# Group 2's second-layer routing and the shared units behind the block loop, and the first page pair's results

## What is computed

```
x = x + attention(ctx, layernorm(x), mask)            # 8 heads, 77 keys
x = x + experts0(layernorm(x))                        # 8 experts, 2 per token, and a shared one
x = x + depool(layernorm(x), ctx): rmsnorm(...) @ W_in.T + b_in + scanned patches
x = x + experts1(layernorm(x))                        # 32 experts, 6 per token, and a shared one

experts1:  scores = sigmoid(x @ gate.T)
           s = scores + bias; the best 4 of 8 groups of experts; then the best 6 experts
           w = 2.5 * scores[best] / sum(scores[best])
           out = sum_e w_e * relu(x @ up_e.T)**2 @ down_e.T + relu(x @ shared_up.T)**2 @ shared_down.T
```

## Time and profile before

| | |
|---|---|
| median of three runs | 887.16 us |
| profiled execution, its own time | 888.47 us |
| its span, first to last instruction | 886.6 us |
| busy: PE, DVE, ACT, POOL | 722.6, 416.7, 273.0, 308.5 us |
| mean granted TensorE clock | 0.903 |
| scatters on POOL: rows_in 96, rows_out 114 | 93.5 and 112.9 us |

### The profile page before, as it was taken

The page is one execution under the profiler, slowest core; times in us unless marked ns, Lnnn a source line. Parts: engine busy times, 40 slices in busy tenths (PEclk is TensorE's granted clock), DMA queues, the critical chain, the costliest instruction groups (busy, mean ns, idle before and its releaser), DMA issues.

```text
span 886.6 us, 14153 instructions
## 1 busy us (share of the span) xinstructions
PE 722.6 (82%) x4526; PEld 631.4 (71%) x4526; DVE 416.7 (47%) x1615; ACT 273.0 (31%) x620; POOL 308.5 (35%) x322
## 2 busy tenths in 40 slices
PE   3868886389999999999899888866776868787865
PEld 2647776289999999999899877533456757676754
DVE  4998664022333243546644742725104444456563
ACT  2636631022111111222223122321123455445540
POOL 1333307600010111100552354172712656556560
PEclk9898859589999999999999998796978899989998
DMA  8999992231776767755866624242646556587866
GB/s 257 396 296 268 257 252 97 102 125 53 231 231 219 218 221 244 246 169 190 304 218 232 217 89 170 92 166 87 217 154 189 177 158 191 164 288 243 285 215 250
DMA packets 93534, 181.22 MB, mean 204 GB/s; under 512 B 9857, under 2 KB 54998, under 8 KB 93182
## 3 DMA queue, kind: packets, MB, share of 16 engines
q1 hardware_dynamic: 78048, 138.67, 50.9%
q0 software_dynamic: 13344, 38.68, 11.6%
q10 hardware_dynamic: 2046, 2.71, 1.0%
HBM read 134.07 MB, written 65.62 MB: 225 GB/s over the span
## 4 chain that ended last, share of the span: by engine, by line
PE 56%; DVE 16%; issue 10%; another core or an unknown queue 6%; DMA 4%; ACT 3%; POOL 3%; SPq 1%; DVEq 0%; POOLq 0%; ACTq 0%
PE PB L618 16%; PE PB L655 11%; PE PB L632 5%; PE PB L825 4%; PE PB L816 4%; PE PB L763 3%; POOL rows_out L1930 3%; PE PB L777 2%; PE PB L804 2%; DMA X<-in_x 2%; PE PB L684 1%; PE PB L600 1%; DMA MEM<-rows_out 1%; DVE WK L1256 1%
## 5 line engine op out<-in xcount | busy, mean ns | idle before, releaser
L618 PE MATMUL PB<-XT,MEM 128*128 128x128 f32 x1584 | 185.9, 276 | 1.1 <-issue 1.1
L618 PEld LDWEIGHTS PB<-XT,MEM 128*128 128x128 f32 x1584 | 181.7, 193 | 1.5 <-issue 1.3
L1882 POOL DMA_INDIRECT sorted_y<-WK x36 | 34.5, 958 | 279.0 <-DVE WK L1470 279.0
L1891 POOL DMA_INDIRECT rows_in<-MEM x96 | 93.5, 974 | 65.1 <-DVE MEM L1674 36.6
L655 PE MATMUL PB<-MEM,WK 128*128 x432 | 99.7, 380 | 3.3 <-DVE MEM L1646 1.9
L825 PE MATMUL PB<-MEM,WK 128*128 x228 | 67.6, 424 | 32.0 <-DVE WK L1823 26.1
L655 PEld LDWEIGHTS PB<-MEM,WK 128*128 128x128 f32 x432 | 79.3, 190 | 13.2 <-issue 3.9
L1930 POOL DMA_INDIRECT rows_out<-WS,MEM x58 | 56.7, 977 | 64.4 <-ACT WS L1045 49.2
L825 PEld LDWEIGHTS PB<-MEM,WK 128*128 128x128 f32 x228 | 42.2, 207 | 41.2 <-issue 36.9
L1930 POOL DMA_INDIRECT rows_out<-MEM x56 | 56.2, 1003 | 40.5 <-ACT MEM L1045 25.7
L939 ACT ACTIVATE XT<-PB 128x256 f32<-128x256 f32 x52 | 19.8, 381 | 162.2 <-PE PB L600 134.2
(11 more groups left out here) (280 smaller groups left out, 1255.4 us busy)
## 6 DMA issues: line engine op xcount, KB each, us to landing
MEM<-in_w SPq DMA_DIRECT2D x36, 896.0 KB
rows_in<-in_consts SPq DMA_DIRECT2D x32, 600.0 KB, 12.2
MEM<-in_w SPq DMA_DIRECT2D x36, 512.0 KB
MEM<-rows_in SPq DMA_DIRECT2D x58, 300.0 KB
MEM<-rows_out SPq DMA_DIRECT2D x16, 768.0 KB, 7.0
MEM<-in_w SPq DMA_DIRECT2D x32, 256.0 KB, 2.8
MEM<-in_w SPq DMA_DIRECT2D x2, 3072.0 KB, 18.9
sorted_x<-MEM SPq DMA_DIRECT2D x1, 5070.0 KB, 39.7
```

Source lines behind the costliest of these rows:

```text
L618: t = e.matmul(o[:, to:to + P], UPW[m][i % (3 - m)][:, k, c * P:(c + 1) * P], XT[:, n % 2, k, :], start=(k == 0), stop=(k == 1))
L1882: e.indirect_dma_start(out=DY, out_offset=bass.IndirectOffsetOnAxis(ap=DEST[:, i:i + 1], axis=0), in_=YS[:, i % 2, :], in_offset=None).the ...
L1891: e.indirect_dma_start(out=DX1, out_offset=bass.IndirectOffsetOnAxis(ap=SLOT1[:, i, j:j + 1], axis=0), in_=XR[:, i, :], in_offset=None).th ...
```

## The change

Four things are changed.

- Group 2's `t1` and `wi` both stand in item i = 34. `t1` stands inside the first part of up, behind two of its seven columns (`SOON`), `wi` behind the seventh; `t2` moves to item 35. Behind the loop `ro 2` now stands directly behind the last block's down and ahead of the late items, and `rank 2`, then DVE's `shares 2` and `slots 2` as entries of their own, around down late 1 and ahead of `sum a 3`. Rank of group 2 uses banks 4 and 5, no longer 2 and 3, so it doesn't wait for "done0".
- q1 and q2 of group 3 are written in halves: two tiles on ACT, two on DVE ("q1v", "q2v").
- Units 4 and 5 are split: "u" is U alone, "d" is D alone, and DVE's drain of unit 3 is an entry of its own ahead of `left 2` and `t2 3`. The pages stand behind entry 8 instead of 7.
- In the pair loop, down2 of pair 0 comes in step 1 instead of 2, and up2 of pair 0, with its relu and square, is first in step 0, ahead of turn1 of pair 1.

With 36 blocks the list is now: turn late 1, down of the last block, ro 2, up late 0, up late 1, down late 0, rank 2, shares 2, down late 1, slots 2, sum a 3, 0, 1, 2, sum b 3, q1 3, 3, t1 3, wi 3, u 4, q2 3, d 3, drain 3, left 2, t2 3, u 5, ro 3, d 4, 6, rank 3, shares 3, 7, slots 3, left 3, 8, pages 3, 9 to 16.

```diff
+ENDS = {s: s - 2 for s in range(2, NPR + 2)}
+ENDS[1] = ENDS.pop(2)
...
+STEP_AT2 = 0, 1, 1, 2, 3, 4
+SOON = {(SUM_AT[2] + 1, 1)}
 for g_ in range(NR - 1):
-    for k_, at_ in enumerate(STEP_AT):
+    for k_, at_ in enumerate(STEP_AT if g_ < 2 else STEP_AT2):
...
-        ("turn", 1), ("down", -1), ("wi", 2), ("up", 0), ("q2", 2), ("up", 1), ("t2", 2), ("down", 0), ("ro", 2), ("down", 1),
-        ("sum a", 3), 0, ("sum b", 3), ("rank", 2), 1, ("q1", 3), 2, ("t1", 3), ("wi", 3), 3, ("left", 2), ("q2", 3),
-        ("t2", 3), 4, ("ro", 3), 5, ("rank", 3), ("left", 3), 6, 7, ("pages", 3), *range(8, 17))
+        ("turn", 1), ("down", -1), ("t2", 2), ("ro", 2), ("up", 0), ("up", 1), ("down", 0), ("rank", 2), ("shares", 2),
+        ("down", 1), ("slots", 2), ("sum a", 3), 0, 1, 2, ("sum b", 3), ("q1", 3), 3, ("t1", 3), ("wi", 3), ("u", 4), ("q2", 3),
+        ("d", 3), ("drain", 3), ("left", 2), ("t2", 3), ("u", 5), ("ro", 3), ("d", 4), 6, ("rank", 3), ("shares", 3), 7,
+        ("slots", 3), ("left", 3), 8, ("pages", 3), *range(9, 17))
...
 def banks_of(g, name):
-    return (4, 5) if g == 2 and name != "rank" else (2, 3)
+    return (4, 5) if g == 2 else (2, 3)
...
                         for c in range(7 - 3 * m):
+                            if m == 0 and c == 2:
+                                between(n, nb, True)
...
             def step(s, n_pairs):
-                if 0 <= s - 2 < n_pairs:
-                    down2(s - 2)
+                if ENDS.get(s, n_pairs) < n_pairs:
+                    down2(ENDS[s])
+                if s == 0:
+                    up2(s)
                 if s + 1 < n_pairs:
                     turn1(s + 1)
                 if 0 <= s < n_pairs:
-                    up2(s)
+                    if s > 0:
+                        up2(s)
...
-                    for i in range(4):
+                    for i in range(4 if g < 3 else 2):
                         t = e.activation(to[:, i, :], X[:, a + i, :], ACT.Identity, bias=R2[:, a + i:a + i + 1],
...
+                if name in ("q1", "q2") and g == 3:
+                    to = XQ if name == "q1" else XR[:, a:b, 0:D]
+                    q.wait_ge("off" + name[1], g)
...
+                    for i in (2, 3):
+                        t = e.tensor_scalar(to[:, i, :], X[:, a + i, :], RS[:, a + i:a + i + 1], R2[:, a + i:a + i + 1],
+                                            ALU.mult, ALU.add)
+                    t.then_inc(*q.mark(name + "v"))
```

More of the change, by code:

```diff
@@ L248 @@
 for nb_ in BLOCKS:
-    k_ = 2
+    k_ = 3
     for i_ in range(BLOCKS[0], nb_):
-        if i_ - SUM_AT[2] >= STEP_AT[k_]:
+        if k_ < 6 and i_ - SUM_AT[2] >= STEP_AT2[k_]:
             EXTRA[nb_, i_] = [(2, k_)]
@@ L255, with steps_of, tail @@
     TAIL[nb_] = [what for what in (
-        ("turn", 1), ("down", -1), ("wi", 2), ("up", 0), ("q2", 2), ("up", 1), ("t2", 2), ("down", 0), ("ro", 2), ("down", 1),
-        ("sum a", 3), 0, ("sum b", 3), ("rank", 2), 1, ("q1", 3), 2, ("t1", 3), ("wi", 3), 3, ("left", 2), ("q2", 3),
-        ("t2", 3), 4, ("ro", 3), 5, ("rank", 3), ("left", 3), 6, 7, ("pages", 3), *range(8, 17))
+        ("turn", 1), ("down", -1), ("t2", 2), ("ro", 2), ("up", 0), ("up", 1), ("down", 0), ("rank", 2), ("shares", 2),
+        ("down", 1), ("slots", 2), ("sum a", 3), 0, 1, 2, ("sum b", 3), ("q1", 3), 3, ("t1", 3), ("wi", 3), ("u", 4), ("q2", 3),
+        ("d", 3), ("drain", 3), ("left", 2), ("t2", 3), ("u", 5), ("ro", 3), ("d", 4), 6, ("rank", 3), ("shares", 3), 7,
+        ("slots", 3), ("left", 3), 8, ("pages", 3), *range(9, 17))
         if not isinstance(what, tuple) or what[1] != 2 or what[0] in rest_
-        or {"q2": "wi", "left": "rank"}.get(what[0]) in rest_]
-def steps_of(n, nb):
+        or what[0] in ("shares", "slots", "left") and "rank" in rest_]
+def steps_of(n, nb, soon=False):
     i = n - EARLY
-    return EXTRA.get((nb, i), ()) if i >= BLOCKS[0] else STEPS.get(i, ())
+    if i < BLOCKS[0]:
+        return [s for s in STEPS.get(i, ()) if (s[0] == 2 and (i, s[1]) in SOON) == soon]
+    if soon:
+        return ()
+    return EXTRA.get((nb, i), ())
 def banks_of(g, name):
-    return (4, 5) if g == 2 and name != "rank" else (2, 3)
-def tail(nb, turn, up, down, mid, up1, down1):
+    return (4, 5) if g == 2 else (2, 3)
+def tail(nb, turn, up, down, mid, up1, down1, drain):
     late = EARLY + nb
@@ L282, in tail @@
                 down(late + i)
+            elif name == "u":
+                up1(i)
+            elif name == "d":
+                down1(i)
+            elif name == "drain":
+                drain(i)
             else:
@@ L635, in up, with between @@
                     between(n, nb)
-            def between(n, nb):
-                for g, k in steps_of(n, nb):
+            def between(n, nb, soon=False):
+                for g, k in steps_of(n, nb, soon):
                     if k in (1, 2, 3, 4) and n + 1 < EARLY + nb + LATE:
@@ L994, in block_iteration @@
                             mid(g, name, 6, 7)
+                    for g, k in steps_of(n, nb, True):
+                        mid(g, NAMES[k], 6, 7)
                     gates(n, nb)
@@ L1035, in act_program, with relu @@
             number1 = e.value_load(PAGES, min_val=0, max_val=P)
+            def relu(s):
+                q.wait_ge("bu", s)
+                q.wait_ge("bd", s - 3)
+                e.activation(HT1[:, s % 3, :, :].rearrange("p b c -> p (b c)"), PB[:, 4 + s % 4, 0:256],
+                             ACT.Relu).then_inc(*q.mark("brl", s))
             def step(s, n_pairs):
-                if 0 <= s - 2 < n_pairs:
-                    r = s - 2
+                if s == 0:
+                    relu(s)
+                if ENDS.get(s, n_pairs) < n_pairs:
+                    r = ENDS[s]
                     q.wait_ge("bd", r)
@@ L1052, in step @@
                                  ACT.Copy).then_inc(*q.mark("bxt", s + 1))
-                if 0 <= s < n_pairs:
-                    q.wait_ge("bu", s)
-                    q.wait_ge("bd", s - 3)
-                    e.activation(HT1[:, s % 3, :, :].rearrange("p b c -> p (b c)"), PB[:, 4 + s % 4, 0:256],
-                                 ACT.Relu).then_inc(*q.mark("brl", s))
+                if 0 < s < n_pairs:
+                    relu(s)
             for s in range(-1, COMMON):
@@ L1737, in page_experts, with drain @@
                 e.tensor_copy(PAGES, EV[0:1, 1:2]).then_inc(*q.mark("pgs"))
-            def down1(n):
+            def drain(n):
                 c, g = UNITS[n]
@@ L1755, in end0, with drain_ahead @@
                     left(n, nb)
-                tail(nb, skip, lambda n: hidden(n, nb), lambda n: result(n, nb), behind_blocks, skip, down1)
+                def drain_ahead(n):
+                    if n != 3:
+                        drain(n)
+                tail(nb, skip, lambda n: hidden(n, nb), lambda n: result(n, nb), behind_blocks, skip, drain_ahead, drain)
             started = len(means)
@@ L1807, in dve_program, with products @@
             running = [None]
+            def products(s):
+                ht = HT1[:, s % 3, :, :].rearrange("p b c -> p (b c)")
+                q.wait_ge("brl", s)
+                e.tensor_tensor(ht, ht, PB[:, 4 + s % 4, 0:256], ALU.mult).then_inc(*q.mark("bh", s))
             def step(s, n_pairs):
@@ L1813, in step @@
                         q.wait_ge(f"w1{j}", 8 * j + 7)
+                if s == 0:
+                    products(s)
                 for k in range(0 if s < 0 else s + 3, min(s + 4, n_pairs)):
```

26 lines of the change are left out of this document (16 added, 10 removed).

## The result

The changed kernel takes 896.97 us (median of 20 runs, 889.37 to 901.09) against 887.93 us for the kernel before in the same comparison (20 runs, 878.86 to 898.59): a ratio of 1.0108, 95% interval 1.0084 to 1.0133. It is slower by 1.1%, outside the range of 868 to 891. The profiled run took 896.35 us, span 894.5 us. Group 3's slots pass the point at which rival D was said to decide, and the unit that part 5 was to gain is lost, as D says; more is lost than D had priced.

What follows compares the result with a forecast made beforehand. The pair loop was taken to start when the shared units are through, which runs of scatters delay by slowing PE. Terms -0.4 - 3.45 - 1.0 = -4.85 against the profiled 888.5 gave 883.65, median 882.3, range 868 to 891.

Steps and rivals of the forecast that it cites:

- rival D: Behind the block loop, group 2's run meets units, turn and product together: slots 7 us later, 889 to 893, chance 0.13.
- part 5: Units behind group 3's slots: PE has one unit more behind the run's start, last unit 3.45 us sooner, or 0.
- part 2: Router and slots of group 2, behind the block loop: slots end at 557.5 instead of 571.6, 14 us sooner.
- part 1: Group 2's turn and product in one block-loop item: loop ends 0.6 us later, bounds 0 and 3.5.
- part 4: Group 2's scatters meet group 3's turn and product: group 3's slots end at 616.9, term 0.4 us, bounds -4 and +8.
- part 6: First pair's products earlier in the pair loop: first scatter 7.1 us behind the turn, 1.0 us gained, bounds 0 and 2.2.
- slow stretch: After 9 to 12 us of back-to-back scatters, PE slows to 1.3 to 1.5 us a matmul until past their end.
- Part 3: Group 3 up to its turn: sums, units and q1 together gain nothing, 0 to 1 us.
- C: Scatters don't slow PE: group 3's product at 576, slots at 598.6, no unit waits; 854 to 870, chance 0.07.
- B: The slow stretch catches less of group 3: its slots end 7 to 12 us sooner, 870 to 876, chance 0.15.
- E: The change does nothing, its gain turned into waiting for the third run's slow stretch: 885 to 889, chance 0.15.

Runs made afterwards that it cites:

- e10: Changed kernel with group 1's last nine scatters held back until group 2's slots are known, then 33 in one run: 905.37 us, ratio 1.0074.
- e1: Changed kernel with POOL's last two runs swapped, group 2's 24 scatters behind group 3's: 902.72 us, ratio 1.013.
- e3: Changed kernel with POOL's two runs behind the block loop broken into gated portions of mostly 3 or 4 scatters: 864.5 us, ratio 0.97.
- e7: e3 with the first run of 32 scatters in portions too: 839.84 us, ratio 0.9458.
- e2: Changed kernel with the 32 expert weight loads cut to 16 of 512 columns: 896.12 us, ratio 1.0068.
- e13: e7 with half of part 6 undone, the first pair's second product back in its old place: 840.39 us, ratio 0.9457.
- e15: e7 measured again, with part 6 as changed: 837.14 us, ratio 0.9403.
- e6: Kernel before, without the change's edits, with POOL's two later runs in portions: 872.66 us, ratio 0.9824.
- e9: e7 without part 6: 840.17 us, ratio 0.9356.
- e11: e9 with gates asking for group 1's last nine scatters in threes; they went as three and six: 840.84 us, ratio 0.937.
- e8: Changed kernel with group 2's 24 scatters back to back but held until group 3's product is through on PE: 896.24 us, ratio 1.0082.
- e12: e6 with part 6 added: 876.79 us, ratio 0.9742.
- after: The kernel with the whole change, against the kernel before: 896.97 us, ratio 1.0108.

## Why the prediction was wrong

Five terms failed: part 2's list of what the stretch meets, which left out nine scatters (8.1 us by e10); part 1's 0.6 us for the end of the loop, which was 4.1; part 4's 21.7 us behind group 3's product, which were 23.7; part 5's gain of 3.45 us, of which nothing came; and part 6's 1.0 us, which no run can tell from nothing.

The profiled run was forecast at 883.65 and is 896.35, 12.7 us more. The slots of group 3 give 5.8 of these (622.7 against 616.9), the units behind them 4.1, the way from the last relu to the first turn 0.6 (9.5 us against 8.9), and the pair loop 2.3 (1.3 longer where 1.0 less was forecast), all rounded.

**The bound and the slow stretch** were right in the main. e1, e3 and e7 show that the late completions follow the runs of scatters, e2 that they don't follow the loads. The 9 to 12 us at pace don't hold for the nine: with the one scatter just before them their run starts at 540.8, and matmuls recorded by 547.1, 6 us into it, are late by 5 us and more (ACT's copy at 552.2 waits 8.3 us). The rule of the Trainium skill ("SBUF — State Buffer", "Who interferes with whom") that TensorE's ports are shared with nobody and a DMA never contends with a compute engine does not account for these traces: scatters alone, spaced out, gave PE 145 matmuls for 104. The runs don't show which resource is shared, so they don't say that the rule on ports is false.

**Part 1** failed in "one wait grows and one goes". The wait for the turn did come, 3.63 us, at the same distance behind the items ahead of it (their hidden product stands at 509.8 against 511.4, the turn at 511.7 against 513.3). But five columns that PE did before it now stand behind it, 2.3 us; the second turn of 1.04 us came into the loop; and q2, whose earlier arrival was to give time back, had kept PE waiting nowhere in the loop before. The last block's result comes 2.4 us later, from items that stood 1.6 us earlier: 4.1 us instead of 0.6, beyond the bound of 3.5. The five columns and the second turn make 3.4 of these; the last down's wait for DVE is another 0.6 longer (2.02 us at 537.2, before 1.38 at 534.8).

```profile
511.69 1.78 PE L687 MATMUL PB<-CC,MEM 128*128 128x128 f32 x8 [3.63 <-ACT XT L962]
513.26 3.40 PE L634 MATMUL PB<-XT,MEM 128*128 128x128 f32 x20
```

**Part 2** failed in its list of what the stretch meets. It followed DVE and PE and left out POOL's nine scatters of group 1, which both kernels issue at the end of the loop. Picks ended at 546.8 (545.1 forecast), but the late items' hidden product came at 555.2 instead of 552 and the slots ended at 564.7 instead of 557.5. e10 takes the nine away and gets 558.05. That this is so near 557.5 is in part luck: from the end of the last block's result the forecast allowed 19.2 us (557.5 less 538.25, the old 537.65 and 0.6), e10 takes 16.5, and its loop ended 3.3 us later than forecast. The slots gained 7 us, not 14. Of the 7.2 us that they are late, 1.8 come from the loop's end and 5.4 from the stretch behind it. The forecast's own rule, the end of a run makes PE late, applied here and was not used: nine scatters last 11.3 us.

**Part 3** held: q1 starts 7.4 us behind the slots, the halves take 1.09 and 0.82 us, and the turn starts 8.9 us behind the slots' end (11.0 forecast).

**Part 4** had the mechanism right: the run's slow stretch held group 3's turn and product. Its slots' end was 5.8 us too early, and by these rows most of that comes in with part 2. Group 2's run began at 565.0 instead of 557.5 and ended at 595.3. DVE got the product's second half at 598.9, 3.7 us behind the run's end and 3.7 us behind the forecast 595.2; the forecast had put it 7.4 us behind the run's end. So the run was 7.5 us later than forecast, and the slow stretch took less of the product's 24 matmuls than 1.3 us each: recorded from 578.4 on and through by 598.9, they had at most 0.85 us each. From there to the slots' end the chain took 23.7 us where 21.7 were forecast (whose terms add up to 21.8).

```profile
599.00:604.00 5.00, 0.00 (x0) 0.00 (x0) 4.48 (x19) 2.17 (x4) 0.00 (x0) 0.50 0.29 105
604.00:609.00 5.00, 4.81 (x18) 3.37 (x18) 2.27 (x10) 1.80 (x6) 0.00 (x0) 0.65 0.00 0
```
```profile
605.95 2.66 PE L783 MATMUL PB<-MEM 128*128 128x512 f32 x4
608.45 1.87 PE L724 MATMUL PB<-G,MEM 128*128 128x32 f32 x16
```

(Columns of the first view as in e3.) Of the 2.0 us (the other pieces are within 0.2 of the forecast), 1.3 lie in the turn, the copies and U5: 4.3 us from q2's end at 604.1 to the router's start at 608.45, where 3 were forecast. PE comes out of the slow stretch at a granted clock of 0.50, the lower of its two levels (1.2 GHz), and has 0.65 in 604 to 609, and U5's four matmuls take 2.66 us instead of 1.88. Another 0.8 us lie between the router's start and the sigmoid's end (3.05 us for 2.3). There stands the table load of 1.28 us, which the forecast had counted around group 2's router only. It ends 0.9 us behind the recorded end of the router's product (611.2 against 610.3), so about that much of it is uncovered. Before, one load at 547.6 served both sigmoids; now the late items' gates (L975) come between the two and change the table at 542.1, and the second sigmoid changes it back. Slots at 622.7 are within a microsecond of the point at which rival D was said to decide (621.7).

**Part 5** failed: the unit was lost. From the third run's start the last relu is 44.3 us away, before 43.7, not 3.45 less. As rival D says, the third run's slow stretch swallows it: relus at 649.1 and 656.9 follow 13.5 and 6.5 us of waiting. One unit fewer is then left than before (four relus from 649.1 on, before five from 647.1), but they come more slowly.

**Part 6** did shorten the way to the first result in this trace, from 9.3 to 7.75 us (7.1 forecast), but the loop was 217.7 us long, before 216.4. The whole edit is worth nothing measurable (e13 to e15).

**The rivals.** D came true in part. Slots past 621.7 and the lost unit are its two losses. Its start is not what happened: U2 and U3 were through at pace (relus at 568.6 and 573.0), since the run began 7.5 us later than D had it, and the product was through at 598.9, half way between the forecast's 595.2 and D's 603 and short of the 600 that D asked for. Its price of 889 to 893 lacked part 1's cost, the nine scatters and the table load. C's premise was wrong. Its size was not far off: once the runs are broken up, the same edits give what C would have given (858 to 865 us). B and E did not occur. The chance of 0.09 for slower went with three slow stretches; a fourth was in the same timeline, where in the kernel before DVE's last add of a late item stands at 549.8 behind 5.1 us of waiting for "remote".

## What to carry to other kernels

If PE's waiters come late for no cause in the rows, look for a run of indirect scatters back to back on POOL and break it up behind steps of the compute before reordering anything around it. Here two runs broken up took the kernel before to a ratio of 0.982 (e6) and the changed kernel from 1.011 to 0.970 (e3); the first run broken up as well gave 0.936 to 0.946 (e7, e9, e11, e13 to e15). The change and three other places for a run (e1, e8, e10) are all slower than the kernel before (1.007 to 1.013). Check in the trace that the gaps are there: a gate behind a step that is already done makes none, and portions of 3 and 4 went out as 6, 10, 13 or, in e12, 20. When a step is priced to meet such a stretch, list what every queue does there, also the part that the change doesn't touch, and count a table load for each time that two functions alternate.

## What the runs showed of the hardware

- With scatters 1.265 us apart, PE's instructions of 0.37 us come up to 2.8 us apart; with a gap of 1.6 to 1.8 us behind every six they run at their pace (342 matmuls in 50 us instead of 158). That so small a gap does away with it in the first run was not expected. Longer portions still show some of it: ACT's relu follows 5.8 us of waiting at 624.8 in e3 (13 scatters) and 5.0 at 594.2 in e7 (14), where 2.2 is the usual, and 20 in e12 bring the whole hole.
- What is late is open. In the first run the starts of PE's matmuls are themselves apart, with the gaps put down to "issue"; in group 2's run their starts are recorded at pace (578.4 to 586.4) and only the waiters are late, by up to 12.5 us. Whether PE lacks instructions or operands or its completions are told late, and which queue or memory fills up, no run here separates.
- The granted clock follows: 0.70 in 130 to 180 us of after, where PE mostly waits from 150 on, and 1.00 in e7. From the group 2 run to the first fetch it is 0.77 and 0.82 in after, 0.92 and 1.00 in e3. A part of the gain of pacing is the clock, not the waits alone.
- The kernel before took a median 887.9, 890.4, 890.7 and 897.6 us in different comparisons, so only kernels of one comparison can be set against each other to better than 1%.
